# Segment softmax of a graph network: forward and backward scans carried in one round, several rows per transfer, one reciprocal as exp(-ln) on ScalarE

## What is computed

```
def _segment_softmax(logits, seg, num_segments):
    m = jax.ops.segment_max(logits, seg, num_segments=num_segments)
    e = jnp.exp(logits - m[seg])
    denom = jax.ops.segment_sum(e, seg, num_segments=num_segments)
    return e / (denom[seg] + 1e-16)
# relational layer, twice:
logits = leaky_relu((out_i @ q + out_j @ k)[:, 0], 0.2)
agg = segment_sum(softmax(logits)[:, None] * out_j, dst)
# attention layer, for each head, with one self loop per node:
e = leaky_relu(alpha_s[src] + alpha_d[dst], negative_slope=0.2)
alpha = exp(e - m[dst]) / (segment_sum(exp(e - m[dst])) + 1e-16)
```

## Time and profile before

| | us |
|---|---|
| median of 3 runs | 4488.05 (4477.16 to 4498.65) |
| the profiled execution | 4457.76 |
| its span on the core | 4456.1 |
| softmax of relational layer 1 | 1822 to 1871 of the span |
| softmax of relational layer 2 | 2454 to 2504 |
| head softmax | 3849 to 4031 |

### The profile page before, as it was taken

The page is one execution under the profiler, slowest core; times in us unless marked ns, Lnnn a source line. Parts: engine busy times, 40 slices in busy tenths (PEclk is TensorE's granted clock), DMA queues, the critical chain, the costliest instruction groups (busy, mean ns, idle before and its releaser), DMA issues. The chain is left out here.

```text
span 4456.1 us, 67687 instructions
## 1 busy us (share of the span) xinstructions
PE 3021.5 (68%) x12366; PEld 1720.8 (39%) x12366; DVE 3403.5 (76%) x10033; ACT 2148.5 (48%) x5598; POOL 2108.6 (47%) x2258
## 2 busy tenths in 40 slices
PE   5956644444445999478999124888888999506886
PEld 1255533333332444123444112555545666303443
DVE  6978868888886888675555785888885666597997
ACT  0057766677662222162222265676765666304554
POOL 0057767777775554006553002555545555103566
PEclk9977767777767999689999555898888999758998
DMA  2079966776672222174331596444445556303333
GB/s 51 2 209 285 285 219 219 231 232 227 225 219 87 65 62 59 45 222 86 62 62 42 135 246 157 121 125 121 126 107 180 194 195 199 112 0 110 114 112 87
DMA packets 622136, 627.73 MB, mean 141 GB/s; under 512 B 168453, under 2 KB 495711, under 8 KB 615589
## 3 DMA queue, kind: packets, MB, share of 16 engines
q1 hardware_dynamic: 574020, 523.79, 39.3%
q0 software_dynamic: 48000, 102.76, 9.4%
HBM read 333.97 MB, written 296.91 MB: 142 GB/s over the span
## 5 line engine op out<-in xcount | busy, mean ns | idle before, releaser
L1410 PE MATMUL r_pM<-r_masked,wr 128*128 128x512 f32 x1600 | 747.3, 620 | 55.2 <-DVE r_masked L1361 55.2
L1361 DVE SCALAR_TENSOR_TENSOR r_masked<-r_typ,r_hT 128x512 f32<-128x512 f32 x800 | 493.9, 688 | 238.4 <-ACT r_hT L1388 189.1
L1410 PEld LDWEIGHTS r_pM<-r_masked,wr 128*128 128x128 f32 x1600 | 307.7, 198 | 424.3 <-issue 293.2
L1252 PE MATMUL e_pY<-ident,e_agg 128*128 128x128 f32 x400 | 134.0, 438 | 367.6 <-DVE e_agg L1127 340.3
L741 POOL DMA_INDIRECT q_rows<-nr,row_x x200 | 258.8, 1294 | 193.3 <-PE q_pT L590 132.3
L2408 POOL DMA_INDIRECT out<-o_base,o_at_o x200 | 239.4, 1197 | 165.1 <-DVE o_base L2449 96.8
L741 POOL DMA_INDIRECT r_xs<-h_tab,r_at_s x200 | 214.8, 1074 | 87.7 <-issue 47.0
L741 POOL DMA_INDIRECT r_xs<-tab,r_at_s x200 | 212.4, 1062 | 89.1 <-issue 48.2
L1252 PEld LDWEIGHTS e_pY<-ident,e_agg 128*128 128x128 f32 x400 | 106.9, 327 | 379.5 <-issue 202.4
L590 PE MATMUL g_pT<-ident,g_hT 128*128 128x128 f32 x400 | 95.9, 384 | 226.7 <-ACT g_hT L1772 176.0
L1006 PE MATMUL na_pZ<-w,na_aT 128*128 128x128 f32 x784 | 158.9, 385 | 117.5 <-ACT na_aT L988 117.4
(11 more groups left out here) (402 smaller groups left out, 8958.4 us busy)
## 6 DMA issues: line engine op xcount, KB each, us to landing
xz<-na_xz SPq DMA_DIRECT2D x49, 1040.0 KB, 5.7
r_typ<-vec_s SPq DMA_DIRECT2D x100, 256.0 KB, 3.4
g_al<-alpha_s SPq DMA_DIRECT2D x100, 256.0 KB, 4.3
na_xz<-in_x SPq DMA_DIRECT2D x49, 512.0 KB, 7.0
tab<-na_x SPq DMA_DIRECT2D x49, 512.0 KB
e_xin<-tab SPq DMA_DIRECT2D x49, 512.0 KB, 6.4
hr<-e_hh SPq DMA_DIRECT2D x49, 512.0 KB, 3.8
zh_s<-e_zh SPq DMA_DIRECT2D x49, 512.0 KB, 4.5
```

What stands on the lines that cost most here:

```text
L1252: pe.matmul(pY[s][:, cols], agg[s][:, cols], g.ident[:, :], start=True, stop=False)
L1361: v.scalar_tensor_tensor(masked[:, r, :], typ[d.slot(4)][:, :], float(r), hT[d.slot(2)][:, :], ALU.is_equal, ALU.mult).then_inc(ev.mk, 1)
L1410: pe.matmul(pM[s][:, :], g.wr[:, layer * R_ + r, :], masked[:, r, :], start=(r == 0), stop=(r == R_ - 1)).then_inc(ev.mm, 1)
```

## The change

`Segments.scan` can now take a forward output (`ahead`) and a backward output (`back`) in one call. Both directions start from the same data: the forward scan gives the value over the segment up to each edge, the backward scan from each edge on. The maximum of both is the segment's maximum. The sum of both counts the edge itself twice, so the edge's own term is subtracted (lines 1568 and 2352 of the new file, in the instruction that adds the epsilon). The first passes of both directions run before the turn, their ends stand in columns 0.. and 32.. (`SECOND = 32`), the turn and the copies take all columns at once, and the rows are scanned in two instructions. The five rounds become three; the number of scans over 200 elements stays the same (24 in `edge_softmax`, 144 in `head_softmax`).

`prepare` gets two memsets, one tensor_scalar and one more reduction. The copies of the ends are one instruction for all vectors. The eight additions of `edge_softmax` become one reduction over a rearranged view and one addition. In `head_softmax` the reciprocal becomes `Ln` and `Exp` with scale -1 on ScalarE. Loads take many rows at a time: 8 rows in the relational stages; 24 and then 12 rows in the head stage, where the 12 are waited for only behind the first round. The store is two transfers of 12 rows, the first of which is issued before the last multiplication. Of the diff:

```
+    def scan(self, v, c, kind, K, data, ahead=None, back=None):
...
+        op0, op1, zero = dict(sum=(ALU.mult, ALU.add, 0.0), max=(ALU.add, ALU.max, -BIG))[kind]
+        keep, more = dict(sum=(g.keep_w, g.more_w), max=(g.keepneg_w, self.moreneg))[kind]
+        kept, mored = dict(sum=(0, 2), max=(1, 3))[kind]
+        first, second = slice(0, K), slice(self.SECOND, self.SECOND + K)
+        if ahead is None:
+            second = first
+        top = K if ahead is None or back is None else self.SECOND + K
+        turn = lambda a: a[:, ::-1]
+
+        def pass_(start):
+            for k in range(K if ahead is not None else 0):
+                last = v.tensor_tensor_scan(ahead[:, k, :], keep[:, :], data[:, k, :], start(first, k), op0, op1)
+            for k in range(K if back is not None else 0):
+                last = v.tensor_tensor_scan(turn(back[:, k, :]), turn(more[:, :]), turn(data[:, k, :]), start(second, k), op0, op1)
+            return last
+
+        c.step(pass_(lambda part, k: zero))
+        if ahead is not None:
+            v.tensor_copy(self.ends[:, first].unsqueeze(2), ahead[:, :, W - 1:W])
+            last = v.tensor_copy(self.whole[:, first], self.totals[:, kept:kept + 1].broadcast_to([P, K]))
...
+        v.memset(self.row_carry[0:top, :], zero)
+        v.tensor_copy(self.row_ends[0:top, :], self.ps[0:top, 0, :])
+        c.step(v.tensor_copy(self.row_whole[0:top, :], self.ps[0:top, 1, :]))
...
+        c.step(pass_(lambda part, k: self.carry[:, part.start + k:part.start + k + 1]))
...
+def wide_rows(a):
+    return a.rearrange("k (p w) -> p k w", w=W)
...
-            for r in range(R_):
-                sp.dma_start(pq[:, r, :], wide(g.pq_s[r, :])).then_inc(s_in, 16)
+            sp.dma_start(pq[:, :, :], wide_rows(g.pq_s)).then_inc(s_in, 16)
...
-            for r in range(R_):
-                c.step(v.tensor_tensor(kq[:, :], kq[:, :], pq[:, r, :], ALU.add))
...
+            c.step(v.tensor_reduce(one[:, :], pq[:, :, :].rearrange("p r w -> p w r"), AX.X, ALU.add))
+            c.step(v.tensor_tensor(kq[:, :], kq[:, :], one[:, :], ALU.add))
...
-            for k in range(3 * NH):
-                sp.dma_start(a_[:, k, :], wide(g.att_s[k, :])).then_inc(s_in, 16)
+            sp.dma_start(a_[:, NH:, :], wide_rows(g.att_s[NH:, :])).then_inc(s_in, 16)
+            sp.dma_start(logit, wide_rows(g.att_s[0:NH, :])).then_inc(s_as, 16)
             sp.wait_ge(s_out, 1)
...
+            sp.dma_start(wide_rows(g.alpha3_s[0:NH, :]), part(a_, 2)).then_inc(s_p, 16)
+            sp.wait_ge(s_out, 2)
+            sp.dma_start(wide_rows(g.alpha3_s[NH:, :]), logit).then_inc(s_p, 16)
...
+            seg.scan(v, c, "sum", NH, logit, part(a_, 1), part(a_, 2))
+            c.step(v.tensor_tensor(c_[:, :, :], part(a_, 1), part(a_, 2), ALU.add))
+            c.step(v.scalar_tensor_tensor(c_[:, :, :], c_[:, :, :], EPS_SM, logit, ALU.add, ALU.subtract))
+            v.tensor_tensor(c_[:, :, :], c_[:, :, :], own, ALU.add).then_inc(s_l, 1)
+            v.wait_ge(s_l, 6)
             c.step(v.tensor_tensor(part(a_, 2), logit, part(a_, 1), ALU.mult))
+            v.sem_inc(s_out, 1)
...
+            a.wait_ge(s_l, 4)
+            a.activation(part(a_, 1), c_[:, :, :], ACT.Ln).then_inc(s_l, 1)
+            a.wait_ge(s_l, 5)
+            a.activation(part(a_, 1), part(a_, 1), ACT.Exp, scale=-1.0).then_inc(s_l, 1)
```

More of the change, by code:

```diff
@@ L1452, in prepare @@
         g = self.g
+        v.memset(self.ends[:, :], 0.0)
+        v.memset(self.whole[:, :], 0.0)
         v.tensor_reduce(self.totals[:, 0:1], g.keep_w[:, :], AX.X, ALU.min)
         v.tensor_reduce(self.totals[:, 1:2], g.keepneg_w[:, :], AX.X, ALU.add)
-        c.step(v.tensor_reduce(self.totals[:, 2:3], g.more_w[:, :], AX.X, ALU.min))
-    def scan(self, v, c, kind, K, out, data):
+        v.tensor_reduce(self.totals[:, 2:3], g.more_w[:, :], AX.X, ALU.min)
+        c.step(v.tensor_scalar(self.moreneg[:, :], g.more_w[:, :], -1.0, BIG, ALU.add, ALU.mult))
@@ L1463, in scan @@
[L1463 to L1469, removed]
-        v.wait_ge(self.turned, n + 1)
-        v.memset(self.row_carry[0:K, :], zero)
@@ L1481, in scan @@
-        c.step(v.tensor_copy(self.carry[:, 0:K], self.ps[:, 2, 0:K]))
-        for k in range(K):
-            last = v.tensor_tensor_scan(way(out(k)), way(mask[:, :]), way(data(k)), self.carry[:, k:k + 1], op0, op1)
-        c.step(last)
-    def turns(self, pe, Ks):
+        op0, op1, zero = dict(sum=(ALU.mult, ALU.add, 0.0), max=(ALU.add, ALU.max, -BIG))[kind]
+        keep, more = dict(sum=(g.keep_w, g.more_w), max=(g.keepneg_w, self.moreneg))[kind]
+        kept, mored = dict(sum=(0, 2), max=(1, 3))[kind]
@@ new lines, in scan @@
+        c.step(pass_(lambda part, k: zero))
+        if ahead is not None:
+            v.tensor_copy(self.ends[:, first].unsqueeze(2), ahead[:, :, W - 1:W])
+            last = v.tensor_copy(self.whole[:, first], self.totals[:, kept:kept + 1].broadcast_to([P, K]))
+        if back is not None:
+            v.tensor_copy(self.ends[:, second].unsqueeze(2), back[:, :, 0:1])
+            last = v.tensor_copy(self.whole[:, second], self.totals[:, mored:mored + 1].broadcast_to([P, K]))
+        last.then_inc(self.ends_done, 1)
@@ L1487, in turns @@
+        last.then_inc(self.row_done, 1)
+        v.wait_ge(self.back, n + 1)
+        c.step(v.tensor_copy(self.carry[:, 0:top], self.ps[:, 2, 0:top]))
+        c.step(pass_(lambda part, k: self.carry[:, part.start + k:part.start + k + 1]))
+    def turns(self, pe, tops):
         g = self.g
-        for n, K in enumerate(Ks):
+        for n, K in enumerate(tops):
             pe.wait_ge(self.ends_done, n + 1)
@@ L2330, in _ @@
             v.wait_ge(s_l, 3)
-            seg.scan(v, c, "sum", NH, of(a_, 1), of(a_, 0))
-            c.step(v.tensor_tensor(part(a_, 2), part(a_, 1), each(g.last_w, NH), ALU.mult))
-            seg.scan(v, c, "back", NH, of(c_, 0), of(a_, 2))
-            c.step(v.tensor_tensor(c_[:, :, :], c_[:, :, :], own, ALU.add))
-            c.step(v.tensor_scalar(c_[:, :, :], c_[:, :, :], EPS_SM, None, ALU.add))
-            c.step(v.reciprocal(part(a_, 1), c_[:, :, :]))
+            seg.scan(v, c, "sum", NH, logit, part(a_, 1), part(a_, 2))
[3 more added lines that the diff above has]
+            v.wait_ge(s_l, 6)
             c.step(v.tensor_tensor(part(a_, 2), logit, part(a_, 1), ALU.mult))
+            v.sem_inc(s_out, 1)
             v.tensor_tensor(part(a_, 0), own, part(a_, 1), ALU.mult).then_inc(s_out, 1)
```

76 lines of the change are left out of this document (34 added, 42 removed).

## The result

| | before | after |
|---|---|---|
| median, us (7 runs each) | 4484.96 (4470.82 to 4498.65) | 4440.57 (4431.53 to 4457.96) |
| ratio after / before, 95% | | 0.9916 (0.9899 to 0.9933) |
| span of the profiled execution | 4456.1 | 4438.7 |
| softmax of relational layer 1 | 48.04 | 42.89 |
| softmax of relational layer 2 | 48.85 | 42.88 |

Faster by 0.84% (0.67 to 1.01%), 38 us by the ratio. The forecast was 4441 us with 4405 to 4466 around it. That the median lies within 1 us of 4441 is luck: the sum was taken off a median of three runs, 4488, that seven runs put at 4485, and the gain by the ratio is 38 us where 46.6 were forecast. A stage is measured here from its ScalarE table load, which comes first in each, to the first work of the next stage. The three stages got shorter by 45.2 us (46.6 predicted).

What follows compares the result with a forecast made beforehand. Three softmax stages, 281 us, were taken as one serial chain of transfers and VectorE between barriers. Gains of 18.4 + 12.4 + 15.8 = 46.6 us, off a median of 4488, gave 4441 us, range 4405 to 4466.

Steps and rivals of the forecast that it cites:

- One chain in three stages: Three softmax stages, 281 us: transfer in, VectorE with short hops, transfer out, nothing beside them; time taken off comes off the execution.
- The heads' computing: Head softmax: column copies 1.4 us, merged maxima round 3.8, end of the heads with its round 13.2; 18.4 us gained.
- The relational stages' computing: Both relational softmax stages: merged rounds, one reduction for eight additions, one column copy; 6.2 us each, 12.4 us gained.
- The upper bound of 3.5: Relational stages' strided reduction: 3.5 us were each read to cost twice, a loss of 0.7 us; 1.8 was taken.
- Transfers: Loads and store of the three stages: heads' load 7.8 us, store 6.6, layers 0.7 each; 15.8 us gained.
- Rival B: Transfers of the three stages run at full speed, 324 GB/s both ways: gain 50 us, 4438 us; chance 0.14.
- the estimate of 20 us: Gain of the four transfers by the skill's 341 GB/s for 1 MB; the whole change would then give 51 us.
- Prepare at nothing: Two memsets, a tensor_scalar and a reduction, about 1 us for each stage, lie beside the loads and cost nothing.
- A: The forecast itself for the whole program: 4430 to 4450 us around 4441; chance 0.62.
- C: New instructions dear: reduction 3.5 us, logarithm twice the exponential, wide turns 0.5, transfers at today's rate; gain 31, 4457 us; 0.14.
- D: Three-dimensional transfers spread over 8 engines instead of 16, 131 GB/s: gain shrinks to 19 us, 4469 us; chance 0.06.
- E: Transfers on four engines or fewer; four, 65 GB/s, give a loss of 32 us, 4520 us; chance 0.04.

## Why the prediction held, point by point

- **One chain in three stages**: held for the stages, whose idle times and instructions add up to their gain. For the program it is shown less sharply. The stages lost 45.2 us; the two ratios show 38 us (30 to 45) and 37 us (29 to 45), so that 45.2 stands at the upper end of both. Two other stages were longer in the first profile of the changed kernel, which the prediction had named as a sign of being wrong; but the interaction stage took 633.1 us without the change too, and the node stage 483.1 with it. The rest of the program was 4177 and 4188 us in two profiles of before and 4175 to 4205, 4187 in the mean, in the ten with the change or a part of it; whether a few us of cost hide in that spread was not settled.
- **The heads' computing**: 18.4 predicted; from the mask's start to the end of the last multiplication 148.99 became 130.84, **18.15**. The round at 27.60 (27.5 by the pieces), ScalarE's pair at 4.50 (4.5) and the copies are right term by term. The logarithm costs what the exponential does, the lower bound.
- **The relational stages' computing**: 12.4 predicted, **9.6** measured (5.15 and 5.97 us of stage less 0.37 and 1.17 of load). The step that failed is "The reduction reads with a step of 200 elements ... I take 1.8": it measured 3.01, so this edit wins nothing (-0.2) instead of 1.0 in each stage. The prediction had named a reduction over 3 us as a sign of being wrong, and this one is. The other 0.4 us were not traced to one term. The reason given, that scans read backward as fast as forward, does not bear on it: a step of one element back stays in its neighbourhood, one of 800 bytes never does. The upper bound of 3.5 had held the case.
- **Transfers**: 15.8 predicted, **17.4** measured: the heads' load 9.28 (7.8), the store 6.6 (6.6), the layers' loads 0.4 and 1.2 (0.7 each). Two terms were mis-sized, with opposite signs. One is the rate of full engines when loading: 262 GB/s had come from dividing 212 by a share of 0.81, as if full engines read 1.00; they read 1.11 and moved 342 GB/s in the middle of the load, so that 2.46 MB take 7.2 us and not 9.4. For the store, 324 GB/s were taken and 321 measured. The other is the fixed part: 9.87 less 7.2 is 2.7 us, where 1.9 was taken, and the layers' loads took 5.77 and 6.02 us, not 5.4. Of the second layer's 1.2 about 1 us is the one long issue in that profile of before. Rival B's 324 both ways was nearer to the rate; the estimate of 20 us that hung on the page's figure came out 2.6 too high. The Trainium skill (DMA: Bandwidth & Descriptors, section Bandwidth) has 341 GB/s for 1 MB; with pieces of 800 bytes the middle of the load agrees (342), and the store stays below it (321).
- **Prepare at nothing**: held. Its seven instructions end at 3868.0 and the mask starts at 3876.32.
- **Rivals**: B's rate with A's time. C's dear reduction came true for one of its four parts, 2.4 us of the 15.8 by which its parts differ from A's. D and E did not occur; the experiment shows E's rate (62 GB/s, where 65 had been taken), and D's was not measured. The two errors, 2.8 us too much in the layers and 1.6 too little in the transfers, have opposite signs, and so the sum stands only 1.4 us from the stages: that closeness, too, is in part luck.

## What to carry to other kernels

Where one engine and its transfers are a single chain between two barriers, a sum over start-to-start pitches from the timeline can come out within a few per cent, even for instructions that are rearranged (18.4 against 18.15 us in the heads). What went wrong here were the terms that no row priced: an operation that reads memory in a new pattern, and transfers at a rate and a fixed part not seen before. A reduction over a rearranged view is not free: adding contiguous halves was a third cheaper. Wait only for the rows that the next instruction needs, which gave 6.0 us at the load here, more than the larger transfer's 3.3; and look at the number of partitions in a transfer: a load cut into 124 and 4 instead of 128 cost 36 us.

## What the runs showed of the hardware

- Reading 1600 elements with a step of 800 bytes: 3.01 us instead of 1.82. Writing with a step of 32 bytes: 3.04 us instead of 2.31 for 8 x 200 elements.
- GpSimd's subtraction of 128 x 2400 (5.33 us) beside VectorE's scans of two inputs made those 5.0 us longer, all of it in one scan (5.54 us).
- Transfers of 12 and 24 rows in pieces of 800 bytes load at 342 GB/s once under way (317 with the start) and store at 321; issued one row at a time, at 0.47 us an issue, they load at 212 GB/s. The load cut into 124 and 4 partitions ran at 62 GB/s with a share of 0.27, and SyncE itself was held for 34 us.
- VectorE's reciprocal costs 15.15 us for 2400 elements a partition, ScalarE's logarithm and exponential together 4.50.
